# An adaLN and mixture-of-experts kernel: numerators added by DMA, squares added by GpSimd, more buffers

## Time and profile before

| | us |
|---|---|
| median of 3 runs | 4682.92 |
| lowest and highest | 4679.94, 4685.01 |
| span of the profiled execution | 4682.9 |
| TensorE busy in it | 4475.7 |
| VectorE busy in it | 2567.2 |
| ScalarE busy in it | 1789.8 |
| GpSimd busy in it | 722.8 |

### The profile page before, as it was taken

The page is one execution under the profiler, slowest core; times in us unless marked ns, Lnnn a source line. Parts: engine busy times, 40 slices in busy tenths (PEclk is TensorE's granted clock), DMA queues, the critical chain, the costliest instruction groups (busy, mean ns, idle before and its releaser), DMA issues.

```text
span 4682.9 us, 60901 instructions
## 1 busy us (share of the span) xinstructions
PE 4475.7 (96%) x19862; PEld 3545.7 (76%) x19863; DVE 2567.2 (55%) x2765; ACT 1789.8 (38%) x2596; POOL 722.8 (15%) x934
## 2 busy tenths in 40 slices
PE   6777999999999999999999999999999999999998
PEld 2245877777777877878888888888888888888887
DVE  8999999999999653433233434444341253333432
ACT  5665555555555333232222323334231142222321
POOL 1000000000000017211111112112111121111111
PEclk8888999999999999999999999999999999999999
DMA  6675767767676766754344545555552254444543
GB/s 226 235 263 184 274 241 268 251 223 282 240 268 226 270 212 190 251 182 111 95 131 112 170 112 160 171 166 150 182 168 57 61 186 145 112 112 116 161 109 61
DMA packets 247928, 835.08 MB, mean 178 GB/s; under 512 B 28160, under 2 KB 61056, under 8 KB 222976
## 3 DMA queue, kind: packets, MB, share of 16 engines
q1 hardware_dynamic: 172944, 572.77, 34.5%
q0 software_dynamic: 47728, 160.07, 15.5%
q10 hardware_dynamic: 27136, 100.67, 5.8%
HBM read 652.40 MB, written 181.01 MB: 178 GB/s over the span
## 4 chain that ended last, share of the span: by engine, by line
PE 80%; DVE 10%; issue 4%; ACT 3%; DMA 2%; POOL 0%; ACTq 0%; DVEq 0%; POOLq 0%; SPq 0%
PE ps L1593 34%; PE ps L1457 22%; PE ps L1607 16%; PE ps L1526 3%; PE ps L1479 1%; PE ps L1582 1%; DVE work L969 1%; DVE work L975 1%; DMA work<-rows_dram,row_idx 1%; PE ps L1477 1%; PE ps L1467 1%; DVE work L996 1%; DVE work L998 1%; DVE work L972 1%; DVE work L1002 1%
## 5 line engine op out<-in xcount | busy, mean ns | idle before, releaser
L1593 PE MATMUL ps<-halves 128*128 128x512 f32 x7152 | 1698.6, 393 | 3.5 <-DVE halves L1356 2.8
L1593 PEld LDWEIGHTS ps<-halves 128*128 128x128 f32 x7152 | 1338.5, 189 | 279.9 <-DVE halves L1356 3.1
L1457 PE MATMUL ps<-halves 128*128 128x512 f32 x6144 | 1450.2, 395 | 13.7 <-issue 12.5
L1457 PEld LDWEIGHTS ps<-halves 128*128 128x128 f32 x6144 | 1154.1, 189 | 287.2 <-issue 47.8
L1607 PE MATMUL ps<-halves 128*128 128x512 f32 x3576 | 834.9, 389 | 1.3 <-DVE halves L1372 1.3
L1607 PEld LDWEIGHTS ps<-halves 128*128 128x128 f32 x3576 | 671.1, 188 | 140.9 <-DVE halves L1372 1.6
L1356 DVE TENSOR_TENSOR halves<-ps,halves 128x1024 fp32r<-128x1024 f32 x150 | 183.7, 1225 | 905.2 <-ACT halves L852 905.2
L1351 DVE TENSOR_TENSOR halves<-work,halves 128x1024 fp32r<-128x1024 f32 (+1 forms) x320 | 440.2, 1433 | 83.6 <-ACT halves L856 83.3
L852 ACT ACTIVATE halves<-ps 128x1024 fp32r<-128x1024 f32 x150 | 154.0, 1027 | 862.4 <-PE ps L1593 862.4
L576 POOL DMA_INDIRECT out<-work,add_idx x149 | 249.8, 1677 | 1417.3 <-DVE work L1378 1382.2
L856 ACT ACTIVATE halves<-work 128x1024 fp32r<-128x1024 f32 (+1 forms) x320 | 369.1, 1229 | 67.0 <-PE ps L1607 56.5
(11 more groups left out here) (186 smaller groups left out, 3674.4 us busy)
## 6 DMA issues: line engine op xcount, KB each, us to landing
halves<-split_dram SPq DMA_DIRECT2D x512, 512.0 KB, 5.6
work<-expert_w SPq DMA_DIRECT2D x192, 1024.0 KB, 5.5
split_dram<-halves ACTq DMA_DIRECT2D x32, 1024.0 KB, 4.9
plain<-shared_w SPq DMA_DIRECT2D x32, 512.0 KB, 3.2
gated_dram<-work ACTq DMA_DIRECT2D x32, 512.0 KB, 4.1
work<-side_t ACTq DMA_DIRECT2D x32, 512.0 KB, 5.6
work<-x_t ACTq DMA_DIRECT2D x32, 512.0 KB, 3.7
ratio_dram<-work ACTq DMA_DIRECT2D x32, 512.0 KB, 4.2
```

The costliest lines, as they stand in the source:

```text
L1457: last = pe.matmul(bank(k % 4), w, op[:, part], start=(c == 0 and w is w_hi and op is hi), stop=(c == CB - 1 and w is w_lo))
L1593: last = pe.matmul(ps_h[:, a * 512:a * 512 + 512], xp[:, xk * P:(xk + 1) * P], wp[:, rhs], start=(xk == 0 and xp is xhi and wp is whi[q]), ...
```

## The change

- **Buffers.** The loaded blocks get four buffers RL instead of two, the stored rows two RS, the squares two SQ, and the third term one W for each l (W_of). SyncE's waits and the steps of the ratio's loads follow (ratio_step: two a step from step 0 for the first four, the others at STEP_L[o - 4] + 3). Semaphore o_out becomes a pair.
- **Results in W.** The scaled result is written to W_of[l] and no longer to N, the first Newton step goes to F and the second to N. So ACT need not wait for a store before it writes N, but euk waits for the store of the unit before from the same W_of[l].
- **Squares.** In halves 0 to 6 (folded) ScalarE writes the square of o = 0 to R, GpSimd adds those of o = 1 to 5 to it (fold_square), and TensorE sums R at the step of o = 5, then o = 6 and 7 as before: three matmuls with ones instead of eight. Half 7 keeps eight.
- **Numerators.** In the units 8 to 31 other than 15, 23 and 31 (these are *prompt*), GpSimd issues a DMA that adds G to W_of[l] in SBUF (add_numerator), in place of the sum on VectorE. The scaling of l = 0 moves behind the forward scan of the numerator of l = 1, that of l = 1 behind the one of the next unit's l = 0. These scans overwrite G, and wait for the DMA. They move behind the backward scan of the denominator. Prompt units add on VectorE, and scale at once.
- **Steps around them.** In such units VectorE's fill(1) and fill(4) move between the scans of the denominator, fill(3) and fill(7) behind the Newton steps. On ScalarE the store of the gated block, with the load of the next side_t behind it, comes after the numerator's edge of l = 1, and the exponential of the next side (side_exp) after fill(7).
- TensorE's numerator for units 0 to 7 has one increment less. The scratch for GpSimd's DMA descriptors is set to 4096 bytes a partition (SCRATCH).

```diff
+ALONE = 2 * UNITS_PER_HALF
+SCRATCH = 4096
+FOLDED = 6
...
+        W_of = (W, sb("second", SEQ)[:, :])
...
-        XL, RL, Z, T = [Z0, Z1, XL0, XL1], [RL0, RL1], [Z0, Z1], SQ
+        more = sb("more", 4 * HALF)
+        RL2, RL3, RS1, SQ1 = (more[:, i * HALF:(i + 1) * HALF] for i in range(4))
+        XL, RL, Z, T = [Z0, Z1, XL0, XL1], [RL0, RL1, RL2, RL3], [Z0, Z1], SQ
+        RS_OF, SQ_OF = [RS, RS1], [SQ, SQ1]
...
+        def folded(h):
+
+            return not final(h)
...
+        def prompt(u):
+
+            return u % CB == CB - 1
+
+        def added(n):
+
+            later = [v for v in range(2 * ALONE, n + 1) if not prompt(v // 2)]
+            return 16 * len(later)
...
+            def fold_square(h, o):
+
+                pool.wait_ge(s["sq"], h * CB + (o + 1))
+                if o > 1:
+                    pool.wait_ge(s["sq_folded"], h * (FOLDED - 1) + (o - 1))
+                apart(pool)
+                pool.tensor_tensor(R, R, SQ_OF[o % 2], ALU.add).then_inc(s["sq_folded"], 1)
+
+            def add_numerator(u, l):
+
+                n = u * 2 + l
+                pool.wait_ge(s["wv_done"], n + 1)
+                pool.wait_ge(s["nb"], n + 1)
+                pool.dma_start(W_of[l], G, accum_op=ALU.add).then_inc(s["num_added"], 16)
+
             clip(0, 0)
-            with pool.Fori(0, BLOCKS // 2) as v:
+            with pool.Fori(0, ALONE // 2) as v:
                 clip(2 * v + 1, 1)
                 clip(2 * v + 2, 0)
+            for u in range(ALONE, BLOCKS):
+                h, q = (u - ALONE) // UNITS_PER_HALF, u % UNITS_PER_HALF
+                if q == 1:
+                    fold_square(h, 4)
+                if not prompt(u):
+                    add_numerator(u, 0)
+                if q == 1:
+                    fold_square(h, 5)
+                if q == 0:
+                    fold_square(h, 1)
+                    fold_square(h, 2)
+                clip(u + 1, (u + 1) % 2)
+                if not prompt(u):
+                    add_numerator(u, 1)
+                if q == 0:
+                    fold_square(h, 3)
...
                 def euk(l):
-                    if l == 0:
-                        sc.wait_ge(s["ratio"], u + 1)
-                    else:
-                        sc.wait_ge(s["gated_raw"], u + 1)
+                    sc.wait_ge(s["gated_out" if l == 0 else "ratio_out"], u * 16 + 1)
                     apart(sc)
-                    sc.activation(W, side_of[par], ACT.Exp, bias=uu[:, ds(u + l * BLOCKS, 1)]).then_inc(s["euk"], 1)
+                    sc.activation(W_of[l], side_of[par], ACT.Exp, bias=uu[:, ds(u + l * BLOCKS, 1)]).then_inc(s["euk"], 1)
+
+                def store_gated():
+                    sc.wait_ge(s["gated"], u + 2)
+                    sc.dma_start(gated_dram[ds(u * P, P), :], W_of[0]).then_inc(s["gated_out"], 16)
+                    load_side(u + 1, 1 - par)
+
+                def store_ratio(u):
+                    sc.wait_ge(s["ratio"], u + 2)
+                    sc.dma_start(ratio_dram[ds(u * P, P), :], W_of[1]).then_inc(s["ratio_out"], 16)
...
-                edges(0)
+                h_edge(0)
+                if prompt:
+                    n_edge(0)
                 euk(0)
                 sc.wait_ge(s["x_in"], (u + 1) * 16)
                 sigmoid(x_of[par], x_of[par], "sig_steps", u, "sig_x")
                 fill(1)
+                if not prompt:
+                    n_edge(0)
+                if pending:
+                    store_ratio(u - 1)
                 inverse(0)
                 fill(2)
                 fill(3)
-                sc.wait_ge(s["gated"], u + 2)
-                sc.dma_start(gated_dram[ds(u * P, P), :], N).then_inc(s["gated_out"], 16)
-                load_side(u + 1, 1 - par)
-                fill(4)
-                edges(1)
-                euk(1)
+                if prompt:
+                    store_gated()
+                    fill(4)
+                    h_edge(1)
+                    n_edge(1)
+                    euk(1)
+                else:
+                    h_edge(1)
+                    euk(1)
+                    fill(4)
+                    n_edge(1)
+                    store_gated()
                 fill(5)
                 inverse(1)
-                side_exp(u + 1)
+                if prompt:
+                    side_exp(u + 1)
                 fill(6)
                 fill(7)
-                sc.wait_ge(s["ratio"], u + 2)
-                sc.dma_start(ratio_dram[ds(u * P, P), :], N).then_inc(s["ratio_out"], 16)
+                if prompt:
+                    store_ratio(u)
+                else:
+                    side_exp(u + 1)
...
             def out_copy(h, o):
                 sc.wait_ge(s["o_tr"], h * CB + (o + 2))
-                sc.wait_ge(s["o_out"], (h * CB + o) * 16 + 1)
-                sc.activation(RS, OUT_BANK, ACT.Copy).then_inc(s["o_copy"], 1)
+                if h or o >= 2:
+                    sc.wait_ge(out_sem[o % 2], (h * (CB // 2) + o // 2) * 16)
+                sc.activation(RS_OF[o % 2], OUT_BANK, ACT.Copy).then_inc(s["o_copy"], 1)
...
-                            wait(sc, "sums", h * CB + o)
-                            sc.activation(SQ, C1[o], ACT.Square).then_inc(s["sq"], 1)
+                            if folded(h) and o == 0:
+                                wait(sc, "z", h * CB)
+                            elif folded(h) and o > 2 and o < FOLDED + 2:
+                                sc.wait_ge(s["sq_folded"], h * (FOLDED - 1) + (o - 2))
+                            elif o > 2 or not folded(h):
+                                wait(sc, "sums", squares_used(h, o - 2))
+                            else:
+                                wait(sc, "sums", squares_used(h - 1, CB - 3 + o))
+                            sc.activation(R if folded(h) and o == 0 else SQ_OF[o % 2], C1[o], ACT.Square).then_inc(s["sq"], 1)
...
+            def scaled(u, l, par, num, inverse):
+
+                ve.scalar_tensor_tensor(W_of[l], num, neg_gain[:, ds(u, 1)], inverse, ALU.mult, ALU.mult)\
+                    .then_inc(s["gated_raw" if l == 0 else "ratio"], 1)
+                if l == 0:
+                    ve.wait_ge(s["gated_raw"], u + 1)
+                    ve.wait_ge(s["sig_x"], u + 1)
+                    ve.tensor_tensor(W_of[0], W_of[0], x_of[par], ALU.mult).then_inc(s["gated"], 1)
+
+            def unit(u, par, fill, summed_by_pe, prompt, pending):
 
                 fill(0)
                 ve.wait_ge(s["ek"], u + 1)
                 ve.tensor_tensor(EKV, EK, side_of[par], ALU.mult).then_inc(s["ekv"], 1)
-                ve.wait_ge(s["ratio"], u + 1)
                 for l in range(2):
                     n = u * 2 + l
                     at = ds(u + l * BLOCKS, 1)
                     d = decay[:, at].to_broadcast([P, SEQ])
+                    W = W_of[l]
+
+                    def numerator_forward():
+                        if l == 0:
+                            ve.wait_ge(s["ekv"], u + 1)
+                        ve.tensor_tensor_scan(G, d, EKV, 0.0, ALU.mult, ALU.add).then_inc(s["nf"], 1)
+
                     ve.tensor_tensor_scan(F, d, EK, 0.0, ALU.mult, ALU.add).then_inc(s["h_fwd"], 1)
-                    if l == 0:
-                        ve.wait_ge(s["ekv"], u + 1)
-                    ve.tensor_tensor_scan(G, d, EKV, 0.0, ALU.mult, ALU.add).then_inc(s["nf"], 1)
+                    if prompt:
+                        if l == 0 and pending:
+                            ve.wait_ge(s["num_added"], added(n - 1))
+                        numerator_forward()
+                    else:
+                        fill(4 if l else 1)
                     ve.wait_ge(s["h_fwd"], n + 1)
                     ve.wait_ge(s["h_edge"], n + 1)
                     ve.tensor_tensor_scan(F[:, ::-1], d, F[:, ::-1], edge_in[:, 0:1], ALU.mult, ALU.add).then_inc(s["h_bwd"], 1)
-                    fill(4 * l + 1)
+                    if not prompt:
+                        if l or pending:
+                            ve.wait_ge(s["num_added"], added(n - 1))
+                        numerator_forward()
+                    if l == 0 and pending:
+                        scaled(u - 1, 1, 1 - par, W_of[1], N)
+                    if l == 1 and not prompt:
+                        scaled(u, 0, par, W_of[0], N)
+                    if prompt or l == 1:
+                        fill(4 * l + 1)
                     ve.wait_ge(s["euk"], n + 1)
                     ve.wait_ge(s["h_bwd"], n + 1)
                     ve.scalar_tensor_tensor(F, W, cap[:, at], F, ALU.min, ALU.add).then_inc(s["h_all"], 1)
@@ -982,32 +1102,28 @@
                     ve.wait_ge(s["n_edge"], n + 1)
                     ve.tensor_tensor_scan(G[:, ::-1], d, G[:, ::-1], edge_in[:, 1:2], ALU.mult, ALU.add).then_inc(s["nb"], 1)
                     fill(4 * l + 2)
-                    if not summed_by_pe:
+                    if prompt and not summed_by_pe:
```

(39 more changed lines are left out.)

101 lines of the change are left out of this document (55 added, 46 removed).

## The result

The changed kernel takes 4636.1 us (median of four executions, 4627.7 to 4641.7); the kernel before took 4681.4 beside it. The ratio is 0.9904, 95% interval 0.9891 to 0.9918: about 1% faster, clear of the noise, and 4 us from the forecast of 4632. The profiled execution took 4640.1 us against 4682.9. One execution in this document, the profiled one of the kernel without folding, took 5116.5 us at a granted clock of 0.83, so it is left out of that kernel's time and its trace is not read.

The account below looks back on a forecast made before the run. PE was taken as the bound, except DVE at the start of half 0. Squares 25.8 + z stage 27 + numerators 3 - frictions 5 = 50.8 us, from 4682.9 to 4632; 8 in 10: 4610 to 4666.

Parts of the forecast that it names:

- z stage, 27 us: Halves 1 to 7: a second RS buffer removes PE's idle time and slow matmuls around z, gaining 27 us.
- DVE is ready for it: z stage: DVE can use the earlier z, since the scaling of the unit before moves behind step 16; no size.
- Squares, 25.8 us: Folded halves: five fewer matmuls with ones save PE 4.3 us a half, counted in six halves, 25.8 us.
- So PE stays the bound with some 9 us of slack on DVE: Loaded halves: DVE's load is 189 us against PE's 198, so PE still sets the time.
- The frictions of 5 us: Five loaded halves: small margins of the later side_t load and DMA traffic cost 1 us each, 5 us lost.
- What GpSimd costs VectorE, at most 0.74 us an addition: Loaded halves: five GpSimd additions cost DVE at most 5 x 0.74 = 3.7 us a half.
- Rival B: Loaded halves: each GpSimd addition holds DVE its whole length, 1.4 to 4.2 us; middle 4650 us, chance 0.12.
- Rival C, the adding DMA: Loaded halves: DVE waits for the adding DMA, decisive from 13.2 us landing; slower, 4707 or 4762 us, chance 0.08.
- Units 0 to 7, nothing: Units 0 to 7: dropped waits of N for a store and DVE for PE gain nothing, at best 3 us.
- Start of half 0, 3 us: Start of half 0, where DVE is the bound: fewer sums and a moved scaling gain 3 us (0 to 8).
- the signs that the forecast named for being wrong: DVE waits for num_added or ek, scans lengthened over 0.8 us, PE idle in steps 0 to 12, z stage late.
- The distance between the marks: PE's timeline: L1486 of half 0 to L1486 of half 7 was to shrink by about 48 us.

Follow-up runs that it names:

- the additions of no use: The changed kernel without folding, but GpSimd makes as many additions of the same size at the same places, results unused: 4639.0 us, ratio 0.9915.

## Why the prediction was right, and which terms were not

The forecast was 50.8 us; the medians differ by 45.3, the profiles by 42.8, and the time fell in the likeliest case's range. The mechanism was right for z and wrong for the squares, and that the sum still fits is luck in good part. By its steps:

- *z stage, 27 us.* 32.4 in the steps with it. The mechanism was as told for half 4, but two of the edits win it only together. The buffer alone won 14 to 16 us, as VectorE was late as well; the rest without the buffer won nothing, because in that kernel the store was also issued later. "DVE is ready for it" is true because of the moved scaling: without the numerator part the steps with z take 146.6 us instead of 131.8, 14.8 of its 19 us.
- *Squares, 25.8 us.* The size for one half was right: without and with folding, steps 5 to 14 take 63.8 and 59.4 us where no unit runs, 4.4 a half (4.3 forecast). But it was won in half 6 alone.
- *The failed step is "So PE stays the bound with some 9 us of slack on DVE".* The load was nearly right (189.4 to 192.9 us measured against 189). The error was to hold it against the period as a whole. VectorE idles around the z stage, cannot use that time, and has 0.1 to 0.2 us of slack in the last 42 us before the next. There the 4.4 us taken from TensorE are won by nobody, and what an addition takes from VectorE is paid at least in part. The frictions of 5 us became 28: steps 5 to 14 of halves 1 to 6 were forecast at 389.8 - 25.8 = 364.0 and took 392.2. That VectorE decides there is shown by the additions of no use. The kernel without the numerator part (19 us slower) agrees, though it moves the scaling as well.
- *What GpSimd costs VectorE, at most 0.74 us an addition.* About 1 us (1.05 in the first row shown). The addition lasts 1.29 us at its shortest (1.28 in half 6 of the kernel with additions of no use, where VectorE runs nothing beside it) and up to 3.0 beside VectorE, so each holds up the other, VectorE by some 80% of the undisturbed length (1.05 / 1.29). For the additions the rule of the Trainium skill ("SBUF — State Buffer", section "Who interferes with whom") is nearer to this than the forecast was, if it is read with the undisturbed length and not with the one in a disturbed trace. For the clip it isn't: that takes 2.8 us or more and lengthened one VectorE instruction by at most 0.8. Rival B, which rests on the rule, named the right cause for the loaded halves, but priced it at 1.4 to 4.2 us an addition and, as the forecast did, held VectorE's load against the whole period.
- *Rival C, the adding DMA:* 8.3 us to land instead of 6.3, 10.9 at most, still under the 13.2 from which it would decide. Waits of 2.9 us in all, nearly the nothing that was forecast.
- *Units 0 to 7, nothing:* 4.8 us between the two profiles, but a stretch that moves by 3 to 4 us from kernel to kernel by itself. How much of it is the change is open. *Start of half 0, 3 us:* 0.2, since the additions of half 0 take back more than was allowed for them (6.4 us come back without them).

So the total is near the measured one because errors cancel: 23 us more of stalls and 3 less at the start of half 0, against 5.4 more at z, 4.8 in units 0 to 7, 5.4 around the ends of the halves and 2.5 in half 7 and behind it; the last three stood at nothing in the forecast. Why the ends of the halves shrank is not settled. One of the edits, folding in halves 0 to 5, is a net loss of 17 us (4636.1 - 4619.1; 15 by the ratios) that the forecast booked as a gain.

Of the signs that the forecast named for being wrong, three came: scans lengthened by 1.0 us beside additions, waits for num_added (2.9 us), and an idle TensorE in step 11 (0.9 to 2.1 us in halves 1, 2 and 4). The distance between the marks shrank by 35.9 us and not by 48. They pointed at the step that failed, though the time was right.

## What to carry to other kernels

Hold an engine's load against each stretch between two meetings, not against the whole period: an engine that must wait at one meeting can have no slack before the next. When a wait for a store is the last link, look at when the store was *issued*, and behind what, before adding a buffer; one edited line in SyncE's order was worth as much as the buffer and its semaphores. Moving work from a busy engine to an idle one is free only if the idle one does not hold up a third: here 0.9 us saved on TensorE cost about 1 us on VectorE, and in the loaded halves VectorE was the bound.

## What the runs showed of the hardware

- A GpSimd addition of 128 x 512 f32 took 1.28 to 1.29 us undisturbed and 1.3 to 3.0 beside VectorE. Where VectorE's instruction had all its operands in SBUF, it became about 1 us longer (1.27 to 2.32, a scan 2.27 to 3.31); instructions that read PSUM did not (0.74 and 0.68).
- A DMA of 512 KB that adds in SBUF took GpSimd 0.9 us to issue and 4.6 to 10.9 us to land (median 8.3), at a DMA share of 0.82 in the loaded periods.
- A store of 256 KB landed 2.5 to 2.6 us after its issue when it was issued ahead of a pair of weight pieces, and 3.9 to 5.4 us after it when it stood behind them (kernel before, halves 1 to 5).
- After TensorE idled for 3.77 us in half 4, the granted clock was 0.50 for 3.7 us, and a pair of matmuls with ones took 2.07 us instead of 1.02.
